# A fused gated-mixing and int8 kernel on one core: the place tables that order four engines are rewritten

## The reference, cut to what matters

```python
h = einsum('bhid,oi,od->bho', x, weighted_sum, weight)        # x: 4 x 512 x 256 x 4
h = concatenate([h, txt], axis=1)                             # 512 + 77 rows of 256, for each of 4 batches
n = layernorm(h)
hid  = relu(n @ gate_w1 + gate_b1); gate = sigmoid(hid @ gate_w2 + gate_b2)
U, S = n @ U_w, cumsum(n @ V_w, axis=1)
h = h + (gate * U * S) @ out_w + out_b + conv3(n, conv_w)     # three taps along the rows
n = layernorm(h)
q = round(n / (absmax(n) / 127)); qr = round(rhs / (absmax(rhs) / 127))
h = h + (q @ qr) * scales
```

## Time and profile before

| | |
|---|---|
| median of 3 runs | 100.67 us (100.51 to 100.87) |
| the profiled execution's own time | 101.48 us |
| its span, first to last instruction | 99.7 us |
| mean granted TensorE clock, as a share of 2.4 GHz | 0.993 |
| busy: PE, VectorE (DVE), ScalarE (ACT), POOL | 92%, 82%, 77%, 61% |
| DMA moved | 17.35 MB, mean 174 GB/s |

### The profile page before, as it was taken

One profiled execution on the slowest core, in us unless ns is written; L12 is line 12 of the kernel. 1 busy time (PEld: TensorE's weight loads), 2 busy tenths in 40 slices (PEclk: granted clock), 3 DMA queues, 4 the chain that ended last, 5 costly groups with the idle time before them and its releaser, 6 DMA issues.

```text
span 99.7 us, 2113 instructions
## 1 busy us (share of the span) xinstructions
PE 91.5 (92%) x686; PEld 83.6 (84%) x686; DVE 81.8 (82%) x228; ACT 76.3 (77%) x151; POOL 61.1 (61%) x105
## 2 busy tenths in 40 slices
PE   5999997999998999999989979999999888998960
PEld 5888896999696999999979959999997677987750
DVE  3376786479989989899998899999998998997641
ACT  1319756999996999969899989857989999927510
POOL 2000046977356706977876856986958959968900
PEclk9999999999999999999999999999999999999997
DMA  3999992779999998499995995799100340003513
GB/s 62 293 300 365 295 330 89 186 252 319 222 192 187 260 322 181 43 204 247 286 342 156 163 210 151 97 249 180 30 9 0 109 141 6 0 0 105 189 63 127
DMA packets 8137, 17.35 MB, mean 174 GB/s; under 512 B 855, under 2 KB 4799, under 8 KB 8127
## 3 DMA queue, kind: packets, MB, share of 16 engines
q0 software_dynamic: 2880, 10.49, 45.7%
q1 hardware_dynamic: 4815, 6.47, 20.5%
q10 hardware_dynamic: 432, 0.27, 0.9%
HBM read 14.81 MB, written 2.41 MB: 173 GB/s over the span
## 4 chain that ended last, share of the span: by engine, by line
PE 38%; ACT 18%; DVE 14%; DMA 10%; issue 7%; POOL 6%; SPq 5%; POOLq 0%; ACTq 0%
DMA x_sb<-x_dram 10%; PE h_ps L920 6%; PE h_ps L924 6%; PE h_ps L922 6%; PE uvg_ps L986 4%; SPq L357 4%; ACT x_low L539 3%; PE acc_ps L1059 3%; PE h_ps L1015 3%; PE h_ps L1011 2%; DVE amax L823 2%; DVE csum L783 2%; ACT xc L643 2%; ACT tmp L546 2%; POOL rstd L406 2%
## 5 line engine op out<-in xcount | busy, mean ns | idle before, releaser
L920 PE MATMUL h_ps<-w_high,x_high 128*128 128x256 f32 x112 | 33.7, 301 | 0.0
L924 PE MATMUL h_ps<-w_high,x_low 128*128 128x256 f32 x112 | 31.3, 279 | 0.0
L922 PE MATMUL h_ps<-w_low,x_high 128*128 128x256 f32 x112 | 31.3, 279 | 0.0
L406 POOL TENSOR_TENSOR rstd<-mv,exponent 128x2 f32<-128x2 f32 (+2 forms) x21 | 19.0, 982 | 17.6 <-DVE mv L717 17.6
L920 PEld LDWEIGHTS h_ps<-w_high,x_high 128*128 128x128 f32 x112 | 21.1, 188 | 0.8 <-issue 0.5
L922 PEld LDWEIGHTS h_ps<-w_low,x_high 128*128 128x128 f32 x112 | 21.1, 189 | 0.2
L924 PEld LDWEIGHTS h_ps<-w_high,x_low 128*128 128x128 f32 x112 | 21.1, 188 | 0.0
L714 DVE BATCH_NORM_STATS2 stats<-h_ps 128x6 f32<-128x256 f32 (+1 forms) x36 | 13.8, 420 | 3.5 <-PE h_ps L924 2.1
L442 POOL DMA_DIRECT2D x_low<-x_dram x10 | 9.4, 938 | 5.3 <-ACT x_low L539 5.0
L795 DVE SCALAR_TENSOR_TENSOR convT<-xnT,conv_minus,convT 128x255 f32<-128x255 f32 (+1 forms) x24 | 11.9, 540 | 0.3
L481 POOL TENSOR_SCALAR v<-xc,qmul 128x256 f32<-128x256 f32 (+1 forms) x20 | 10.0, 507 | 2.5 <-DVE qmul L827 2.4
(11 more groups left out here) (113 smaller groups left out, 193.9 us busy)
## 6 DMA issues: line engine op xcount, KB each, us to landing
x_high<-x_dram POOLq DMA_DIRECT2D x10, 512.0 KB, 7.0
x_low<-x_dram POOLq DMA_DIRECT2D x10, 512.0 KB, 5.9
x_sb<-x_dram SPq DMA_DIRECT2D x4, 512.0 KB, 8.3
out_dram<-fin SPq DMA_DIRECT2D x8, 256.0 KB
x_sb<-x_dram SPq DMA_DIRECT2D x3, 256.0 KB, 4.3
par_sb<-par_dram SPq DMA_DIRECT2D x1, 325.0 KB, 7.9
txt_sb<-txt_dram SPq DMA_DIRECT2D x1, 308.0 KB
out_dram<-fin SPq DMA_DIRECT2D x4, 77.0 KB
```

The source lines that it names most:

```text
L406: nc.gpsimd.tensor_tensor(out_ap, var_ap, exponent[0:out_ap.shape[0], 0:out_ap.shape[1]], ALU.pow).then_inc(done, 1)
L920: nc.tensor.matmul(h_of(g)[:, t, :], x_high[:, g % RING, kc, at], w_high[:, kc, :], start=(kc == 0 and t == 0), stop=False, skip_group_che ...
L922: nc.tensor.matmul(h_of(g)[:, t, :], x_high[:, g % RING, kc, at], w_low[:, kc, :], start=False, stop=False, skip_group_check=True)
L924: last = nc.tensor.matmul(h_of(g)[:, t, :], x_low[:, g % RING, kc, at], w_high[:, kc, :], start=False, stop=(kc == KC - 1), skip_group_che ...
```

## The change

Both tables and the small ones get new numbers. No helper function changes, no operand, no buffer, no semaphore. The lines of after.py are two lower than those of before.py from L80 on, since two literals are shorter.

```diff
-    turn=(193, 322, 433, 593, 674, 817, 1009, 1017),
+    turn=(225, 339, 449, 593, 721, 817, 1011, 1015),
...
-WARM_AT = {1033: 1, 1036: 1, 1038: 1, 1040: 2, 1042: 2, 1044: 2, 1047: 5, 1048: 7, 1049: 2, 1050: 1, 1051:
-           1, 1052: 1}
+WARM_AT = {1036: 6, 1039: 5, 1042: 3}
```

More of the change, by code:

```diff
@@ L40 @@
[L40 to L46, removed]
-    chip_low0=(-1, 1, 5),
[L48 to L53, removed]
+    stats=(2, 6, 15, 23, 31, 41, 52, 58),
@@ new lines @@
+    rstd=(0, 4, 8, 15, 22, 33, 42, 47),
+    norm=(5, 13, 23, 35, 48, 57, 72, 78),
+    turn=(225, 339, 449, 593, 721, 817, 1011, 1015),
+    move=(7, 17, 26, 39, 51, 60, 76, 80),
+    hidden=(241, 369, 497, 625, 754, 881, 1014, 1020),
+    relu=(9, 20, 36, 42, 62, 66, 81, 83),
+    sums=(8, 16, 26, 32, 44, 50, 62, 65),
+    gates=(-1, 401, -1, 642, -1, 898, -1, 1021),
+    sigmoid=(-1, 22, -1, 44, -1, 67, -1, 86),
+    gated=(-1, 10, -1, 23, -1, 40, -1, 54),
+    high=(24, 25, 46, 47, 69, 70, 88, 91),
@@ L58 @@
[L58 to L65, removed]
@@ L66 @@
-    lscale=(19, 20, 29, 42, 43, 48, 53, 57, 59, 65, 69, 71),
-    turn=(626, 673, 693, 754, 1010, 1014, 1022, 1026, 1032, 1037, 1041, 1045),
-    ints=(42, 47, 55, 73, 77, 80, 88, 95, 97, 99, 103, 104),
-    product=(657, 692, 757, 1011, 1013, 1018, 1027, 1030, 1035, 1039, 1043, 1046),
-    out=(37, 42, 47, 61, 63, 66, 73, 75, 77, 80, 82, 83),
-    fin=(30, 34, 41, 49, 51, 52, 63, 64),
-)
-TXT_AT = dict(turn=289, hidden=321, gates=337, stats=4, uv=13, norm=9, move=12, relu=15,
-              sigmoid=18, rstd=2)
@@ L76 @@
-RHS_AT = dict(turn=370, low=0, round=12, out=17, fold=24, fold_low=55, high=0, fold_high=68)
+    put=(-1, -1, 33, -1, -1, 58, -1, -1, 77, -1, -1, 95),
+    conv=(465, 467, 561, 705, 707, 833, 961, 1012, 1017, 1023, 1028, 1032),
+    mix=(466, 468, 562, 706, 708, 834, 962, 1018, 1019, 1025, 1029, 1034),
+    stats=(21, 22, 27, 38, 39, 47, 56, 63, 64, 70, 74, 78),
+    rstd=(13, 20, 25, 30, 34, 39, 45, 53, 58, 59, 67, 69),
+    centre=(28, 30, 38, 52, 54, 63, 73, 85, 87, 93, 98, 101),
+    keep=(29, 31, 40, 53, 55, 64, 74, 90, 92, 96, 100, 102),
@@ L77 @@
+TXT_AT = dict(turn=305, hidden=337, gates=340, stats=4, uv=12, norm=10, move=12, relu=15, sigmoid=18, rstd=2)
+RHS_AT = dict(turn=338, low=0, round=10, out=13, fold=14, fold_low=54, high=0, fold_high=68)
 DIAG_AT = 3
-WARM_AT = {1033: 1, 1036: 1, 1038: 1, 1040: 2, 1042: 2, 1044: 2, 1047: 5, 1048: 7, 1049: 2, 1050: 1, 1051:
-           1, 1052: 1}
+WARM_AT = {1036: 6, 1039: 5, 1042: 3}
 FIN_ON_DVE = 8
```

31 lines of the change are left out of this document (20 added, 11 removed).

## The result

The change made the kernel slower: 102.78 us median of 4 runs (102.13 to 104.66) against 100.77 for the kernel before beside it, a ratio of 1.0149 (95% interval 1.0100 to 1.0198). A second comparison gave 1.0151 (1.0088 to 1.0214). The forecast was 98.7 us, range 97.6 to 100.4; sign and range are both wrong.

What follows compares the result with a forecast made beforehand. PE was taken to bound the kernel up to 73.6 us, a chain through all four engines behind 88 us. Terms -1.40 - 0.73 - 0.20 + 0.40 - 0.8 + 0.8 = -1.93 us took 100.67 to 98.7 us, range 97.6 to 100.4.

Steps and rivals of the forecast that it cites:

- Head, -1.40: Start of the kernel: PE's waits before `turn` of g0 (-0.77 us) and `gates` of g1 (-0.63 us) go.
- PE sets the pace: Blocks of g2 to g7, up to 73.6 us: PE, busy 52.3 of 53.6 us, sets the pace unless made to wait.
- the copies of g4 come late: Rival at g4's first block: its add lands up to 2.2 us late, giving 101.1 us; chance 0.12 with like losses.
- Middle, -0.93: Blocks of g4 to g7: PE's wait before `q_turn` of j3 goes (-0.73 us), that before `turn` of g4 partly (-0.20).
- all other middle moves at nothing: Middle of the kernel: remaining moves cost 0, their inputs being ready 1 us and more before.
- After the last block, +0.40: Behind the last block: later `sums` of g6 costs +0.15 us, `scale` of j8 before `low` of g6 the rest; bounds 0 and +1.7.
- Statistics of j10, -0.8: Tail on DVE: statistics of j10 go before `out` of j7, so `round` of j10 comes 0.8 us sooner; bounds 0 and -0.9.
- Keep-warm, +0.8: End of PE's work: lot of six costs +0.55 us, five +0.27, three fit under a wait; bounds +0.3 and +1.0.
- a block of g4 late behind a copy: Sign against the forecast: a block of g4 to g7 starts late behind a copy; no size given.
- `hidden` of g7 waiting over 0.5 us for VectorE: Sign against the forecast, behind the last block: PE's `hidden` of g7 waits over 0.5 us for DVE.
- a lower clock: Sign against the forecast: a granted clock that differs; before it was 1.00 in the blocks, 0.94 behind 88 us.
- VectorE did not take the pace: Rival between 20 and 73.6 us: DVE takes the pace and half of head and middle is lost, 99.8 us; chance 0.22.

Runs made afterwards that it cites:

- v1_tail_old: Changed kernel up to the last block of g7, all four engines in the old kernel's order from there on: 102.06 us median, ratio 1.0093.
- u3_warm: Changed kernel with 9 keep-warm matmuls in lots of 1, 2, 2, 2, 2 instead of 14 in lots of 6, 5, 3: 102.24 us, ratio 1.0101.
- c_after: The changed kernel run once more, nothing altered, for a second profile: ratio 1.0151, span of the profile 100.6 us.
- x4_head: Kernel before with the changed order on all four engines up to the first block of g4, old order after: 102.24 us median, ratio 1.0083.
- after: The changed kernel itself, in its first profile: 102.78 us median, ratio 1.0149; the profiled execution took 102.13 us.
- v2: Kernel before up to the last block of g7, the changed kernel's order behind it: ratio 1.0133.
- w2: Changed kernel with, on VectorE, `sums` of g6 back before `scale` of j6 and `low` of g6 before `scale` of j8: 102.72 us, ratio 1.0190.
- u1: Changed kernel with the first add of g4 back ahead of the cast of g5 on GpSimd, and its negation earlier on ACT: 103.96 us, ratio 1.0285.
- u2: Changed kernel with VectorE's `scale` of j6, `sums` of g6 and `low` of g6 back in their earlier places: 103.14 us, ratio 1.0158.
- w1: Changed kernel with `norm` and `move` of g0 on ACT back ahead of the first and second `chip_high` of g2: ratio 1.0273.
- w3: Kernel before with keep-warm in lots of 6, 5, 3 instead of 1, 1, 1, 2, 2, 2: 102.10 us median, ratio 1.0159.

## Why the prediction was wrong, by its steps

**Head, -1.40: the waits went at best, the gain did not come.** Both removed waits are gone in the first profile; the one before `turn` of g0 is back, with 0.49 and 0.44 us, in v1_tail_old and u3_warm, where the first half of g2 landed later than the 15.1 that the step had estimated. The step that failed is another one: it counted a wait of PE as time of the kernel because "PE sets the pace". The head alone measured +0.8%, not -1.4. Its cover was named as data that have landed; that holds for g2 and g3 and not for g4. I had read the DMA share as 0.85 over 53.6 us. That is an average over stretches that differ. Windows of four microseconds of the kernel before:

```profile
40.00:44.00 4.00, 4.00 (x36) 4.00 (x35) 3.63 (x10) 3.82 (x8) 3.74 (x6) 1.00 0.71 106
...
52.00:56.00 4.00, 4.00 (x37) 3.92 (x37) 3.49 (x12) 3.90 (x8) 2.75 (x6) 1.00 0.60 156
...
60.00:64.00 4.00, 4.00 (x36) 4.00 (x36) 3.80 (x12) 3.70 (x7) 3.24 (x6) 1.00 0.56 110
```

and of the changed one:

```profile
40.00:44.00 4.00, 4.00 (x38) 3.96 (x37) 2.81 (x9) 2.83 (x7) 3.92 (x9) 1.00 1.06 251
...
52.00:56.00 4.00, 3.90 (x34) 3.65 (x33) 3.87 (x13) 3.63 (x8) 3.76 (x7) 1.00 1.00 176
...
60.00:64.00 4.00, 4.00 (x36) 4.00 (x35) 3.87 (x9) 3.97 (x10) 2.40 (x6) 1.00 0.69 142
```

Between 20 and 60 us no four microseconds of this profile of the changed kernel are below 0.90; the kernel before has gaps of 0.71 and 0.60. It is tempting to take these gaps for slack that the copies need, and their loss for the cause. The runs do not bear it out. c_after has a window of 0.70 (24 to 28 us) and the same 1.5% of loss. And the head alone, which is slower as well, has the gaps in its own trace, windows of x4_head:

```profile
24.00:28.00 4.00, 4.00 (x28) 2.99 (x26) 3.63 (x11) 3.95 (x8) 1.10 (x2) 1.00 0.77 131
...
52.00:56.00 4.00, 3.78 (x35) 3.55 (x34) 3.87 (x13) 3.93 (x9) 2.94 (x5) 1.00 0.51 75
```

So what the runs show in place of the forecast is that the time which PE saved in the head came back as waits behind it: at the first block of g4 in the changed kernel, before `turn` of g4 and at three more places in x4_head. Why the head makes the kernel not merely equal but slower stays open.

**The rival "the copies of g4 come late" happened,** at a smaller price in the profile than it was given. The add was issued at 31.16 (31.3 forecast) and landed at 39.2, 8.0 us later, between the median and the longest of the earlier trace rows; PE idled 1.0 us there, and by starts, as the prediction counts its waits, it lost 1.4 (from `hidden` of g2 to the next block 2.03 us, before 0.67), where I had put the threshold at a landing at 40.5 and the price at 2.2. The landing at 37.2 that the forecast stood on did not come: the earliest among the profiles with this order of the copies is x4_head's, issued at 31.19 and landed 6.9 us or more later. The 3.2 us estimated from the Trainium skill ("DMA: Bandwidth & Descriptors", Anatomy of one DMA) do not hold for these copies: the quickest add took 5.4 us in this profile.

**Middle, -0.93, and "all other middle moves at nothing".** `q_turn` of j3 no longer waited, as said. But alone the middle costs 2.0%. Its trace shows two of the moves costed at nothing: `q_turn` of j0 three blocks sooner (1.52 us, hidden only by the head), and `scale` of j6 from ahead of to behind the statistics of g7. No run has either of them alone.

**After the last block, +0.40: the sum was mis-sized, and one term was missing.** In the pair of profiles this stretch costs 0.66 us up to `hidden` of g7 and another 0.66 up to `mix` of j9, 1.3 in all, within the bound of 1.7. The delay of `sums` of g6 was sized at 1.7 and became 2.2, 0.75 of it by the slow `nstep`. PE's own new order ahead of `hidden` of g6, which puts it 1.3 to 1.5 us later (after, v2, w2), had no term at all; I had listed the move and not priced it. With it in place, `sums` waits for PE as soon as VectorE no longer delays it (w2), which limits what undoing VectorE's part can give. No run undid both with the rest of the change kept.

**Statistics of j10, -0.8.** `round` of j10 came 0.86 sooner (91.06 against 91.92), but that is close to the forecast by luck: counted from the end of `scale` of j9, as the step does, it started 3.39 us after it; before that had been 3.97, and the forecast was 3.2. That is a gain of 0.6, and the rest of the 0.86 comes from stages ahead. The last it waited for was `scale` of j10, stretched by the `fin`, and not the `fin` itself. And `q_turn` of j10 came only 0.32 sooner, as it stands behind `ffn` of j9, and that now waits for `out` of j8 behind `scale` of j10. I had followed the chain of j10 and not the queue of PE. Alone the move is worth +0.6%.

**Keep-warm, +0.8.** By the trace the first lot is free in this order, where +0.55 was forecast; the second costs the forecast 0.25; the third costs nothing, as forecast (from `ffn` of j10 to `ffn` of j11 2.27 us, before 2.29). Singly they measured +0.0, +0.3 and +0.1%. The sum is too high by these, too low if the three at once cost 1.6%. The clock did play a part in one execution, but not through the lots: they act behind 88 us, while the fall came at 80, behind waits that the change itself made.

**Summed up:** the step that failed first is "PE sets the pace": waits taken from PE were counted as time. Up to the last block PE was 1.6 us ahead in the first profile (0.58 of it by the start of that execution), 1.5 in c_after, 0.6 to 0.9 in v1_tail_old and u3_warm and 2.3 and more in w2_sums; the forecast had 2.3. No run turned any of it into time, and the body without the new tail measured +0.9%. The second is the tail's +0.40, mis-sized and short of a term: the new tail alone measured +1.3%. Of the signs that I had named against the forecast three came: a block of g4 late behind a copy, `hidden` of g7 waiting over 0.5 us for VectorE, and, in one of ten executions, a lower clock. VectorE did not take the pace: its busy time between 20 and 73.6 us is 49.2 us, before 49.4.

**What stays open.** Why most executions of the changed kernel are 1 us longer than its first profile with no fall of the clock. A late landing of g2's load is a candidate: u3_warm's profile, span 100.5 with the clock at 1.00 throughout, has the wait before `turn` of g0 back and the last block 0.66 us later. But no such execution of the changed kernel itself was profiled. And why time less span, 1.7 to 1.9 us in every execution of a kernel with the old lots, is 2.4 to 3.1 in six of ten of the changed kernel and in a few executions of u1, u2, v2, w1 and w2. All of these have the new tail and the new lots together; neither u3 (new tail, nine matmuls) nor w3 (old tail, new lots) shows it in any of six.

## What to carry to other kernels

A wait of the busiest engine is worth its length only if everything behind it can come sooner as well: follow the steps that it must meet next, on every engine and in the queue of copies, before calling one engine the pace. When an order is rewritten, price every step that is moved ahead of a late one on the same queue, on all engines, also where the mover itself costs nothing; and look for what the moved step frees or fills for others. A swap that seems to be the culprit may guard against a second wait of the same length (u1_copies), so undo it alone before blaming it, and look whether the undo brings a new wait (w1_norm). Where a view names who ended a wait, check against the code whether that step was asked for.
